# An adaLN block on one Trainium2 core: transposed modulation in the prologue, the gate's bias added to x by an accumulating DMA, scales by half tile

## The reference

```python
mod = (_silu(L0_c) @ L0_wmod).reshape(L0_c.shape[0], 6, 1, -1)
sa, ca, ga, sb, cb, gb = (mod[:, 0], mod[:, 1], mod[:, 2], mod[:, 3], mod[:, 4], mod[:, 5])
ga = (2 * (ga >= 0) - 1) * jnp.maximum(jnp.abs(ga), 0.25)
gb = (2 * (gb >= 0) - 1) * jnp.maximum(jnp.abs(gb), 0.25)
h = _layernorm(x, axis=-1) * (1 + ca) + sa
x = x + ga * _L0_attn_ref(h, ...)
h = _layernorm(x, axis=-1) * (1 + cb) + sb
x = x + gb * _L0_ffn_ref(h, L0_ffn_weight, L0_ffn_bias)
```

## Time and profile before

| | |
|---|---|
| time, median of 3 runs | 390.24 us (390.23 to 390.87) |
| the profiled execution | 389.05 us, span 387.2 us from first to last instruction |
| busy, of the span | PE 83%, DVE 79%, ACT 57%, POOL 53% |
| mean granted TensorE clock | 0.942 of full |
| moved by DMA | 68.10 MB, mean 176 GB/s |

### The profile page before, as it was taken

The page is one execution under the profiler, slowest core; times in us unless marked ns, Lnnn a source line. Parts: engine busy times, 40 slices in busy tenths (PEclk is TensorE's granted clock), DMA queues, the critical chain, the costliest instruction groups (busy, mean ns, idle before and its releaser), DMA issues.

```text
span 387.2 us, 6242 instructions
## 1 busy us (share of the span) xinstructions
PE 321.5 (83%) x2302; PEld 244.5 (63%) x2302; DVE 306.0 (79%) x500; ACT 219.8 (57%) x498; POOL 203.9 (53%) x123
## 2 busy tenths in 40 slices
PE   2940075785999999999899998979999989985994
PEld 0100012574798887788787776868887777664883
DVE  1893497699864699698979787999887899799733
ACT  2001858573835777787594969677876776110310
POOL 2004886909928549554973868294939372600000
PEclk9995569589999999999999999999999999998999
DMA  7998445769945884959394869566955951102032
GB/s 264 387 407 318 95 70 212 124 215 298 200 156 124 260 148 179 186 197 216 112 239 158 203 163 246 137 172 164 268 123 182 210 139 69 42 0 109 25 139 81
DMA packets 23156, 68.10 MB, mean 176 GB/s; under 512 B 2563, under 2 KB 2692, under 8 KB 19022
## 3 DMA queue, kind: packets, MB, share of 16 engines
q1 hardware_dynamic: 14982, 51.67, 37.6%
q0 software_dynamic: 7392, 14.68, 23.9%
q10 hardware_dynamic: 752, 1.36, 1.2%
HBM read 50.50 MB, written 17.20 MB: 175 GB/s over the span
## 4 chain that ended last, share of the span: by engine, by line
PE 43%; DVE 28%; issue 9%; ACT 7%; POOL 6%; DMA 4%; SPq 1%; DVEq 0%; POOLq 0%; ACTq 0%
PE ps L574 8%; PE ps L575 8%; PE ps L579 8%; PE ps L557 4%; DVE DD L1002 3%; DVE XL L965 3%; PE ps L655 3%; DVE amax L984 3%; PE ps L531 2%; DVE WL L972 2%; PE ps L570 2%; DMA v_bc<-mod_scratch 2%; DVE X L1009 2%; POOL U L326 2%; POOL U L328 2%
## 5 line engine op out<-in xcount | busy, mean ns | idle before, releaser
L326 POOL TENSOR_TENSOR U<-U,c_bc 128x1024 f32<-128x1024 f32 x32 | 78.3, 2448 | 54.2 <-ACT U L391 54.2
L574 PE MATMUL ps<-WH,XH 128*128 128x512 f32 x256 | 101.7, 397 | 0.7 <-ACT XH L375 0.7
L575 PE MATMUL ps<-WL,XH 128*128 128x512 f32 x256 | 101.5, 396 | 0.0
L375 ACT ACTIVATE XH<-ps 128x512 fp32r<-128x512 f32 x64 | 37.9, 592 | 81.6 <-PE ps L557 81.5
L328 POOL TENSOR_TENSOR U<-U,sb_bc 128x1024 f32<-128x1024 f32 x32 | 76.8, 2400 | 2.5
L965 DVE TENSOR_TENSOR XL<-ps,XH 128x512 fp32r<-128x512 f32 x64 | 44.0, 687 | 39.8 <-ACT XH L375 39.7
L579 PE MATMUL ps<-WH,XL 128*128 128x512 f32 x256 | 69.7, 395 | 1.3 <-DVE XL L965 1.3
L391 ACT ACTIVATE U<-X,nmr,rstd 128x512 f32<-128x512 f32 x64 | 48.5, 808 | 27.9 <-DVE nmr L980 27.8
L579 PEld LDWEIGHTS ps<-WH,XL 128*128 128x128 f32 x256 | 48.5, 190 | 12.4 <-DVE XL L965 2.0
L575 PEld LDWEIGHTS ps<-WL,XH 128*128 128x128 f32 x256 | 48.8, 191 | 11.1
L402 ACT ACTIVATE unused<-X 128x512 bf16<-128x512 f32 x64 | 39.4, 618 | 28.5 <-POOL X L317 27.6
(11 more groups left out here) (209 smaller groups left out, 404.1 us busy)
## 6 DMA issues: line engine op xcount, KB each, us to landing
X<-in_x SPq DMA_DIRECT2D x16, 1024.0 KB, 4.9
out<-X SPq DMA_DIRECT2D x15, 1024.0 KB, 5.8
X<-mod_scratch POOLq DMA_DIRECT2D x14, 1024.0 KB, 10.1
X<-in_wmod SPq DMA_DIRECT2D x4, 1024.0 KB, 9.6
c_bc<-mod_scratch SPq DMA_DIRECT2D x6, 256.0 KB, 7.7
sb_bc<-mod_scratch SPq DMA_DIRECT2D x6, 256.0 KB, 7.8
...
```

The source lines that it names most:

```text
L326: nc.gpsimd.tensor_tensor(a, a, spread(c_bc[:, b % 2, :]), ALU.mult).then_inc(u_done, 1)
L574: M(bank, XH[:, n % 2, r], WH[:, b % 2, k, :], start=False, stop=False)
L575: M(bank, XH[:, n % 2, r], WL[:, b % 2, k, :], start=False, stop=False)
```

## The change

Modulation (PE): the weight block is now the stationary operand and the condition the moving one, so each of four rows comes out as 128 channels x 8 batches for four chunks; all of them lie in one PSUM bank. DVE forms gates, C, SB and biases on 128x32 into the tile TA. A row that all partitions need is made by PE (`spread`): the column of TA, repeated 128 times as the stationary operand, against the identity. V, C and SB for batch 0 come this way. The rows for memory are transposed back by PE (`rows_of`) and written in three DMAs; batches 1 to 7 read C and SB from there, as before. The two rows that only the head rows need (CA, SA) are formed behind products 0 and 1 from a stationary operand that holds each batch 16 times (`head_rows`), and no longer pass through memory.

Group 0: V is added to its first half by DVE and to the second by GpSimd; the first half is also modulated by DVE, straight from the PSUM banks (`first_modulate`). Half 0 goes through maxima, scales and grid before half 1.

The gate's bias: the matmul of ones with G2 is gone from all 64 products, with G2 and its loads. In its place GpSimd issues one accumulating DMA a group (`bias_by_dma`), which adds GBIAS to x once the group is normalised; `add_tile` of a group's first tile waits for it. The attention row is added for group g+3 behind `modulate(g)`, where it was g+2 ahead of it.

Scales: TS and REC on 128x32 for each half, where there was one pair on 128x64 for the group. Statistics and normalisation of a group stand 10, 9 and 7 slots ahead (`stage`), where they stood 13, 11 and 9. Attention starts at slot 9 (8 before).

The product begins with L651, without a matmul of ones ahead of it, as in the diff, which is cut to its core:

```diff
-V, C, SB, GB, GBIAS, CA, SA, GA, GBH, GBL = range(10)
-FIRST, LAST = -17, TILES * GROUPS
-BEGIN, PERIOD = 8, 15
-AFTER = 36 + 14
+V, GBIAS, C, SB, GB, GA = range(6)
+ROWS = 6
+LAST = TILES * GROUPS
+BEGIN, PERIOD = 9, 15
+AFTER = BEGIN + 2 * PERIOD + 12
...
-        G2 = sb("G2", [P, 2, D], F32R)
...
+        TA = sb("TA", [P, NC, ROWS, B])
...
+            sp.dma_start(idf[:], ident).then_inc(small_in, 16)
             load_mod(0)
...
             load_x(0)
+            sp.dma_start(Wd[:], w.rearrange("(c p) k -> p c k", p=P)).then_inc(w_in, 16)
             load_mod(1)
+            load_x(1)
             load_mod(2)
-            sp.dma_start(Wd[:], w.rearrange("(c p) k -> p c k", p=P)).then_inc(w_in, 16)
             load_mod(3)
-            load_x(1)
+            sp.wait_ge(rows_cp, 1)
+            sp.dma_start(mod_dram[V], first_rows[:, 0, :]).then_inc(v_out, 16)
+            load_x(2)
+            load_mod(4)
             load_mod(5)
-            sp.wait_ge(mod_mm, 1)
-            load_mod(4)
+            sp.wait_ge(rows_cp, 2)
+            sp.dma_start(mod_dram[GBIAS], first_rows[:, 1, :]).then_inc(gbias_out, 16)
+            load_x(3)
             sp.dma_start(xs[:], xh).then_inc(xs_in, 16)
             sp.dma_start(row_bc[:], lna[None, :].to_broadcast([P, D])).then_inc(lna_in, 16)
-            load_x(2)
-            sp.wait_ge(mod_mm, 3)
+            sp.dma_start(BD[:], BDs).then_inc(bd_in, 16)
+            sp.wait_ge(rows_cp, 3)
+            sp.dma_start(mod_dram[C:ROWS].rearrange("w b d -> (w b) d"), mod_rows).then_inc(scratch_out, 16)
+            sp.wait_ge(scratch_out, 16)
+            mod_row(c_bc[:, 1, :], 1, C, c_in[1])
+            mod_row(sb_bc[:, 1, :], 1, SB, sb_in[1])
+            load_x(4)
+            sp.wait_ge(wt_mm, NC)
+            sp.dma_start(Wb[:], chunked(WqT)).then_inc(wq_in, 16)
+            sp.wait_ge(mod_mm, 5)
+            sp.dma_start(Wv[:], chunked(WvT)).then_inc(wv_in, 16)
+            sp.wait_ge(mod_mm, 6)
...
             def add_attn_bias(g):
-                b = g // 2
+                pool.wait_ge(v_rows, 1)
+                pool.wait_ge(x_in[g], 16)
+                for h in range(g == 0, 2):
+                    a = X1[:, g, HALF * h:HALF * (h + 1), :]
+                    nc.gpsimd.tensor_tensor(a, a, spread(v_bc[:]), ALU.add).then_inc(x1_done, 2 if g == 0 else 1)
+            def add_row(g, which):
+                nc.gpsimd.dma_start(X1[:, g % XSLOTS, :, :],
+                                    mod_dram[which, g // 2:g // 2 + 1, :].unsqueeze(1).to_broadcast([P, TILES, D]),
+                                    accum_op=ALU.add).then_inc(x_added[g % XSLOTS], 16)
+            def sum_by_dma(g):
+                if g == 2:
+                    pool.wait_ge(v_out, 16)
                 pool.wait_ge(x_in[g % XSLOTS], 16 * (g // XSLOTS + 1))
-                if b > 0:
...
-                pool.wait_ge(v_in[0], 16)
-                for h in range(2):
-                    a = X1[:, g % XSLOTS, HALF * h:HALF * (h + 1), :]
-                    nc.gpsimd.tensor_tensor(a, a, spread(v_bc[:]), ALU.add).then_inc(x1_done, 1)
+                add_row(g, V)
+            def bias_by_dma(g):
+                if g == 0:
+                    pool.wait_ge(gbias_out, 16)
+                pool.wait_ge(z_done, TILES * (g + 1))
+                add_row(g, GBIAS)
...
+            add_attn_bias(0)
+            add_attn_bias(1)
+            scale_weights(0, Wfirst, 0, HALF)
+            scale_weights(0, Wfirst, HALF, NC)
+            bias_by_dma(0)
+            modulate(0)
+            sum_by_dma(2)
+            scale_weights(1, Wsecond)
+            sum_by_dma(3)
+            for g in range(1, GROUPS):
                 modulate(g)
-                if g == 0:
-                    scale_weights(0, Wfirst)
-                    scale_weights(1, Wsecond)
+                bias_by_dma(g)
                 if g % 2 == 1 and 3 <= g < GROUPS - 1:
                     scale_weights((g + 1) // 2, Wscaled)
+                if g + 3 < GROUPS:
+                    sum_by_dma(g + 3)
...
+            def spread_row(dst, bank, mm, signal, n):
+                act.wait_ge(mm, n)
+                A.copy(dst, ps[:, bank, :]).then_inc(signal, 1)
+            def copy_rows(dst, bank, n):
+                act.wait_ge(rows_mm, n)
+                A.copy(dst, ps[0:dst.shape[0], bank, :]).then_inc(rows_cp, 1)
             act.wait_ge(t_ok, 1)
             A.activation(tsc[:, 4, :], tsc[:, 3, :], ACT.Sqrt).then_inc(t_sqrt, 1)
...
+            spread_row(v_bc[:], V0_BANK, v_mm, v_rows, 2)
+            sums(0, 0)
+            copy_rows(first_rows[:, 0, :], V_ROWS, 1)
+            sums(0, 1)
+            deviations(0, 0)
+            deviations(0, 1)
+            copy_rows(first_rows[:, 1, :], GBIAS_ROWS, 2)
+            normalise(0, 0)
+            spread_row(c_bc[:, 0, :], C_BANK, c_mm, c_rows, 1)
+            normalise(0, 1)
+            spread_row(sb_bc[:, 0, :], S_BANK, s_mm, s_rows, 1)
+            sums(1, 0)
+            for k in range(NC):
+                weight_high(0, k, W_FIRST_BANKS[k])
+            copy_rows(mod_rows, S_BANK, 3)
+            sums(1, 1)
+            high_part(0)
+            deviations(1, 0)
...
             def modulation(i):
                 pe.wait_ge(wmod_in[i], 16)
+                for n in range(NC):
+                    for k in range(NC):
+                        m = M(mods(i)[:, n, :], mod_w[i][:, k, n * P:(n + 1) * P], cE[:, k, :],
+                              start=k == 0, stop=k == NC - 1)
+                m.then_inc(mod_mm, 1)
+            def spread(bank, which, b, signal):
+                for n in range(NC):
+                    m = M(ps[:, bank, n * P:(n + 1) * P], TA[:, n, which, b:b + 1].to_broadcast([P, P]), idf[:],
+                          start=True, stop=True)
+                m.then_inc(signal, 1)
...
+            def head_rows(i, bank):
+                pe.wait_ge(wmod_in[i], 16)
                 for k in range(NC):
-                    m = M(mods(i), cE[:, k, :], mod_w[i][:, k, :], start=k == 0, stop=k == NC - 1)
+                    m = M(ps[:, bank, :], cH[:, k, :], mod_w[i][:, k, :], start=k == 0, stop=k == NC - 1)
                 m.then_inc(mod_mm, 1)
+            def rows_of(bank, w0, w1, signal):
+                for n in range(NC):
+                    m = TR(ps[0:(w1 - w0) * B, bank, n * P:(n + 1) * P],
+                           TA[:, n, w0:w1, :].rearrange("p w b -> p (w b)"), idf[:])
+                m.then_inc(signal, 1)
...
-                M(bank, onesr[:], G2[:, b % 2, :], start=True, stop=False)
...
+                if q == 0:
+                    pe.wait_ge(c_heads, 1)
+                    pe.wait_ge(wt_low, NC)
+                    head_rows(4, CA_BANK)
+                elif q == 1:
+                    head_rows(5, SA_BANK)
...
             def gate(i, dst, vec, res, signal):
                 dve.wait_ge(mod_mm, i + 1)
-                TS(gate_sign, mods(i), 0.0, 2.0, ALU.is_ge, ALU.mult).then_inc(dve_step, 1)
+                link(TS(sign, mods(i), 0.0, 0.5, ALU.is_ge, ALU.subtract))
+                link(STT(size, sign, 2.0, mods(i), ALU.mult, ALU.mult))
+                link(TS(size, size, 0.25, 2.0, ALU.max, ALU.mult))
+                link(TT(size, size, sign, ALU.mult))
+                W_.tensor_copy(TA[:, :, dst, :], size).then_inc(dve_step, 1)
                 chain[0] += 1
-                link(W_.tensor_copy(gate_abs, mods(i)))
-                link(STT(gate_abs, gate_sign, -1.0, gate_abs, ALU.add, ALU.mult))
-                link(TS(gate_abs, gate_abs, 0.25, None, ALU.max))
-                link(STT(mrow[dst], gate_sign, -1.0, gate_abs, ALU.add, ALU.mult))
-                link(STT(gate_sign, gate_sign, -1.0, gate_abs, ALU.add, ALU.mult))
-                TT(mrow[res], vec, gate_sign, ALU.mult).then_inc(signal, 1)
...
+                TT(TA[:, :, res, :], size, col[:, vec:vec + NC].unsqueeze(2).to_broadcast([P, NC, B]),
+                   ALU.mult).then_inc(signal, 1)
...
+            def first_modulate():
+                a = U[:, 0, 0:HALF, :]
+                dve.wait_ge(z_done, HALF)
+                dve.wait_ge(c_rows, 1)
+                TT(a, a, spread(C_BANK), ALU.mult).then_inc(u_first, 1)
+                dve.wait_ge(u_first, 1)
+                dve.wait_ge(s_rows, 1)
+                TT(a, a, spread(S_BANK), ALU.add).then_inc(h_first, 1)
...
             def maxima(g, h):
-                dve.wait_ge(h_done, 2 * g + h + 1)
+                if g == 0 and h == 0:
+                    dve.wait_ge(h_first, 1)
+                else:
+                    dve.wait_ge(h_done, 2 * g + h + 1)
                 RED(amax[:, h, :], blocks(U[:, g % 2, HALF * h:HALF * (h + 1), :]), AX, ALU.max,
                     apply_absolute_value=True).then_inc(am_done, 1)
-            def block_scales(g):
-                dve.wait_ge(am_done, 2 * g + 2)
-                TS(s64, amax[:], 64.0 / 7.5, 64e-30, ALU.mult, ALU.max).then_inc(s_done, 1)
```

(48 more changed lines are left out.)

416 lines of the change are left out of this document (190 added, 226 removed).

## The result

The changed kernel takes 395.07 us (median of 4 runs, 394.77 to 395.26), the one before 390.56 beside it. The ratio is 1.0128, with an interval of 1.0105 to 1.0151. The profiled execution spans 393.2 us. Run again later, unchanged, it took 390.96 us (10 runs, 389.31 to 395.20) against 390.30, a ratio of 1.0016 (0.9993 to 1.0040). So the change brings nothing to a loss of 1.3%, and the forecast of 363 us, with 0.92 on faster, is wrong by some 30 us. A ratio compares undisturbed runs alone and can so differ from the quotient of the medians.

What follows compares the result with a forecast made beforehand. The DMA engines were to become the bound by a small margin: 93 us to tile 8, 197 to the last attention addition's landing, 71 to the end, span 361, plus 1.85 beside it: 363 us, range 343 to 380.

Steps and rivals of the forecast that it cites:

- Modulation at 4.2 us, product 0 at 46: Prologue: 4.2 us for each modulation's 16 matmuls; first product near 46 us (44 to 50), 23 us earlier.
- The ramp, tile 8 at 93: From first product to tile 8: shortened from 57.5 to 47 us, tile 8 added at 93 (88 to 103).
- The gate bias by DMA: Steady part: 30 accumulating DMAs instead of 14 make the DMA engines the bound, 18.8 to 20.0 us a group against 17.8.
- 268 us from tile 8 to the end: Steady part and end: 197 us to the last attention addition's landing, including 3 of gaps, then 71 to the end.
- the signs: Whole run: full DMA row, q0 near 190 us, waits on DMAs, first product at 44 to 50, PE below 97%.
- the fourth: Steady part, a sign: ScalarE's sums or DVE's tile addition wait on a DMA, tens of us in all.
- Rival A: Steady part: DMA isn't the bound, additions overlap or x buffers carry the excess; 345 us, chance 0.23.
- The ones row at 0.23 a tile: Each product: removing the ones-row matmul saves 0.23 us a tile, 0.31 at most, 12.7 us over 55 tiles.
- C: Steady part: additions meeting on q0 don't overlap, each costs its landing time; slower than before, 410 us, chance 0.06.
- B: Steady part: DMA is the bound, badly fed because GpSimd waits in order for loads; 386 us, chance 0.14.
- D: Prologue: spreads and gates wait on each other, product 0 at 60; 363 to 376 us; forecast with D 0.55.
- the last term: From tile 49, read at 313.30, to the end: 73.9 us now, less 14 x 0.23, taken as 71.

Runs made afterwards that it cites:

- f2: The changed kernel with its own VectorE order, only the preparation of bias rows and diagonals moved into VectorE's idle time before 14 us: 384.00 us, ratio 0.9812.
- e6: e5 with the C and SB rows of batch 0 made straight from the modulation weights by products of 512 columns: 366.70 us, ratio 0.9359.
- e5: e2 with VectorE's preparation of the bias rows and diagonals done before the first gate: 373.13 us, ratio 0.9577.
- e1: The changed kernel without the sixteen DMAs of the gate's bias (output lacks that bias): 390.52 us, ratio 0.9961.
- e9: e2 without the sixteen DMAs of the gate's bias (output lacks that bias): 381.63 us, ratio 0.9784.
- e4: The kernel before with the new VectorE order, half-tile scales, and scales and normalisation two slots later, from group 2 on: 400.91 us, ratio 1.0286.
- e2: The changed kernel with VectorE's steps spread over the four slots of a group, from group 2 on: 382.28 us, ratio 0.9816.
- e8: e2 with a ones-row matmul of zeros back in each product: 387.98 us, ratio 0.9954.
- e3: The kernel before with its ones-row matmul gone and the gate's bias added by DMA: 392.43 us, ratio 1.0060.

## Why the prediction was wrong, step by step

- **Modulation at 4.2 us, product 0 at 46.** Wrong in size: product 0 came at 57.6 (54.8 again). The row that I priced a pass from, eight halves of 128x128 in 1.05 us, stood in the steady part at a granted clock of 1.00, the 2.4 GHz level. There the price holds: f2's second pass took 3.9 us. But in the first profile all four passes had loads of 333 ns, the duration of the 1.2 GHz level, and took 6.8 to 7.0 us. The forecast saw the lower clock in the prologue, let its range reach to 50 for it and left the passes at the faster price. Against 4 x 4.2 the four passes are 10.8 us longer, of the 11.6 missed; in the repeated profile 8.8, of 8.8. Such a match is closer than it should be, since the spreads took 2.1 us and not 1.1 and other steps less than I gave them. e6, with two of the passes replaced, reached 47.9.
- **The ramp, tile 8 at 93.** The step that cost most. The forecast shortened the ramp from 57.5 to 47 us on the ground that GpSimd would wait less for loads. It does wait less, and the ramp is 64.3 us. I hadn't counted what the diff put into it: 12.1 us of VectorE's preparation, which the kernel before did in its prologue. e5 and f2 show 53.8 and 53.6 us without it, and e1 and e9 about 2 us for the bias DMAs. What keeps e5 and f2 above 47 was not tested.
- **The gate bias by DMA, "the part that decides".** The amounts were right (a share of 0.98; 63.5% of 220 us for 23.51 MB is 5.94 us per MB, against 6.32 forecast). The conclusion was wrong: a share of 1 is not a wait. e1 and e9 took the DMAs out and the pace didn't move. The forecast gave 268 us from tile 8 to the end, and 271 were measured, but for another reason: agreement of that sum is luck and proves nothing for its mechanism. So it is with the signs: the DMA row at 9, 188 us of q0's engine time (47.9% of 393.2) and TensorE at 92% in the middle all came as said, and only the fourth, waits on a DMA of tens of us, could tell a full resource from a bound. It showed none. Rival A was right on the DMA engines and had the same errors elsewhere. The estimate from the Trainium skill, "DMA: Bandwidth & Descriptors", "Anatomy of one DMA — SWDGE (gpsimd) path", of 2.4 us an addition stays refuted as engine time: the trace has 5.94 us per MB.
- **VectorE's order.** Not priced at all, though the diff shows it. With the half-tile scales and the later normalisation it costs 0.267 a tile in the kernel before (e4), and evening it returns 0.198 in the changed one (e2): 11 to 15 us. Together with the 10.7 us of the ramp (f2) this takes back what the earlier start (11.6) and the ones row (4 to 7) give.
- **The ones row at 0.23 a tile.** Half of it: 0.122 (e8), and 0.073 in the old kernel (e3), where DMAs came in its place. TensorE's waits for VectorE take the rest in e8.
- **Rivals.** C, the only one on the slower side, asked for additions that are waited for, and in the changed kernel none is (4.4 us in e3). B's wait grew only in e3. D gave product 0 at 60, close to 57.6, and then kept the short ramp. No rival spoke of VectorE, which stood at 185 of 220 us in the same row as TensorE.

The sum of the misses, against a span of 361: 11.6 us at product 0, 17.3 in the ramp (64.3 against 47), 3.3 from tile 8 on, together 32.2, and 361 + 32.2 is the 393.2 measured. One reading inside the forecast was off by a tile: 313.30 is the addition of tile 48, counted as tiles 8 and 63 are; tile 49 is added at 317.3 in the kernel before, so the last term had 4 us too much.
